# Experts computed only for the tokens that chose them: 32-token slots in four column groups of the array, planned on the chip

## The reference

```python
def _L1_ffn_ref(x, gate_w, routing_bias, w1, w2, w3, sw1, sw2, sw3):
    E = 16; K = 4
    def _swiglu(x, w1, w2, w3):
        a = x @ w1
        return a * jax.nn.sigmoid(a) * (x @ w2) @ w3     # w1, w2: 512 x 1365, w3: 1365 x 512
    gate_out = x @ gate_w + routing_bias
    top_v, top_i = jax.lax.top_k(gate_out, K)
    chosen = jax.nn.one_hot(top_i, E).sum(axis=-2)
    probs = jax.nn.softmax(jnp.where(chosen > 0, gate_out, NEG), axis=-1)
    weights = probs * chosen
    out = _swiglu(x, sw1, sw2, sw3)                       # the shared expert, every token
    for e in range(E):
        out = out + _swiglu(x, w1[e], w2[e], w3[e]) * weights[..., e:e + 1]
    return out
```

## Time and profile before

| | us |
|---|---|
| median of 3 runs | 536.06 |
| profiled execution, device time | 535.71 |
| its span, first to last instruction | 533.7 |
| PE busy / its weight loads | 522.6 / 406.9 |
| DVE / ACT / POOL busy | 425.1 / 337.2 / 8.9 |
| bytes moved | 190.11 MB, mean 356 GB/s |

### The profile page before, as it was taken

One profiled execution on the slowest core, in us unless ns is written; L12 is line 12 of the kernel. 1 busy time (PEld: TensorE's weight loads), 2 busy tenths in 40 slices (PEclk: granted clock), 3 DMA queues, 4 the chain that ended last, 5 costly groups with the idle time before them and its releaser, 6 DMA issues.

```text
span 533.7 us, 7582 instructions
## 1 busy us (share of the span) xinstructions
PE 522.6 (98%) x2672; PEld 406.9 (76%) x2672; DVE 425.1 (80%) x426; ACT 337.2 (63%) x324; POOL 8.9 (2%) x40
## 2 busy tenths in 40 slices
PE   8999799999999999999999999999999999999998
PEld 4665335467878888888888888888888888888886
DVE  6724610167899989889898998989998988989796
ACT  1100100158787878788786877877787877778573
POOL 2000000011000000000000000000000000000000
PEclk9988999999999999999999999999999999999999
DMA  8999999999999999999989999899999999999331
GB/s 338 422 421 421 421 421 422 417 409 416 414 404 414 372 375 348 351 394 337 404 284 380 374 344 384 320 381 339 368 358 356 345 341 395 340 369 350 123 108 70
DMA packets 37032, 190.11 MB, mean 356 GB/s; under 512 B 4090, under 2 KB 4474, under 8 KB 31636
## 3 DMA queue, kind: packets, MB, share of 16 engines
q1 hardware_dynamic: 36816, 189.70, 92.0%
q10 hardware_dynamic: 196, 0.14, 0.1%
HBM read 189.56 MB, written 0.26 MB: 356 GB/s over the span
## 4 chain that ended last, share of the span: by engine, by line
PE 91%; DVE 7%; ACT 1%; issue 1%; DMA 1%; POOL 0%; DVEq 0%; ACTq 0%; POOLq 0%
PE ps L1572 29%; PE ps L1610 23%; PE ps L1576 14%; PE ps L1594 4%; PE ps L1221 3%; PE ps L1385 3%; DVE s_lo L891 2%; PE ps L1414 1%; PE ps L1402 1%; PE ps L1214 1%; PE ps L1283 1%; PE ps L1299 1%; DVE s_lo L903 1%; PE ps L1273 1%; PE ps L1287 1%; PE ps L1545 1%
## 5 line engine op out<-in xcount | busy, mean ns | idle before, releaser
L891 DVE TENSOR_TENSOR s_lo<-w_raw,s_hi 128x1365 fp32r<-128x1365 f32 x136 | 209.1, 1579 | 16.0 <-ACT s_hi L657 15.6
L657 ACT CAST s_hi<-w_raw 128x1365 fp32r<-128x1365 f32 x136 | 180.4, 1337 | 26.3 <-PE ps L1576 13.1
L1572 PE MATMUL ps<-s_hi,xT_hi 128*128 128x512 f32 (+1 forms) x408 | 153.7, 377 | 0.3 <-DVE s_lo L891 0.3
L1572 PE MATMUL ps<-s_lo,xT_hi 128*128 128x512 f32 (+1 forms) x408 | 149.7, 369 | 0.0
L1576 PE MATMUL ps<-s_hi,xT_lo 128*128 128x512 f32 (+1 forms) x408 | 106.6, 369 | 0.0
L903 DVE TENSOR_TENSOR s_lo<-w_raw,s_hi 128x1536 fp32r<-128x1536 f32 x68 | 105.8, 1578 | 0.0
L669 ACT CAST s_hi<-w_raw 128x1536 fp32r<-128x1536 f32 x68 | 90.8, 1343 | 21.4 <-PE ps L1576 18.3
L1572 PEld LDWEIGHTS ps<-s_hi,xT_hi 128*128 128x128 f32 x408 | 76.6, 188 | 17.0 <-DVE s_lo L891 0.5
L1572 PEld LDWEIGHTS ps<-s_lo,xT_hi 128*128 128x128 f32 x408 | 77.0, 189 | 12.5
L1576 PEld LDWEIGHTS ps<-s_hi,xT_lo 128*128 128x128 f32 x408 | 72.7, 189 | 6.0
L1610 PE MATMUL ps<-s_hi,hT_hi 128*128 128x512 f32 (+1 forms) x180 | 72.8, 404 | 0.2 <-DVE hT_lo L1097 0.2
(11 more groups left out here) (249 smaller groups left out, 305.5 us busy)
## 6 DMA issues: line engine op xcount, KB each, us to landing
w_raw<-in_w SPq DMA_DIRECT2D x128, 682.5 KB, 6.2
w_raw<-in_w SPq DMA_DIRECT2D x51, 768.0 KB, 6.1
w_set<-in_w SPq DMA_DIRECT2D x31, 1024.0 KB, 24.5
w_raw<-in_w SPq DMA_DIRECT2D x12, 512.0 KB, 5.8
w_raw<-in_sw SPq DMA_DIRECT2D x8, 682.5 KB, 15.6
wk_sb<-in_wk SPq DMA_DIRECT2D x2, 1024.0 KB, 16.6
wq_sb<-in_wq SPq DMA_DIRECT2D x2, 1024.0 KB, 16.0
gcn_sb<-in_gcn_w SPq DMA_DIRECT2D x2, 1024.0 KB, 13.1
```

Source lines behind the costliest of these rows:

```text
L657: a.copy(s_hi[pair][:, 0:F1], raw[:]).then_inc(hi_ready, 1)
L891: v.tensor_tensor(s_lo[pair][:, 0:F1], raw[:], s_hi[pair][:, 0:F1].bitcast(F32), ALU.subtract).then_inc(lo_ready, 1)
L1572: mm(bank(i + c0 // D)[:, 0:n], xT_hi[:, k], w[:, c0:c0 + n], start=(k == 0 and w is hi), stop=False)
```

## The change

The last stage is written anew, with the rest left nearly as it was.

**Slots.** Work is done in slots of 32 tokens for one expert. Slots 0 to 3 are the shared expert for tokens 0-31, 32-63 and so on. After them come 36 routed slots, always 36: TURNS = 18 turns of two slots, the number that suffices for any choice of the tokens (`most_turns`). A turn has a slot on side b and one on side a.

**The PE work of a slot.** The 1365 columns of w1 and w2 are cut into four groups of 342 (the last is padded from 339 to 342), one for each 32 columns of the array: `up` makes 4 row tiles x 4 groups = 16 matmuls of 32 tokens x 342 for w1, and as many for w2. `down` makes 3 row tiles x 4 groups = 12 matmuls of 512 columns. The four groups' partial sums lie in four sets of 32 PSUM partitions, and `add_slot` adds them and puts them on their tokens with one 128x512 matmul whose stationary operand, `spread`, holds the gates. Everything is fp32; the splitting into hi and lo is gone. `gather_batch` gathers the tokens of four slots at once.

**The weights.** They are used where they land. A ring of two buffers holds one expert each; loads fetch w1 and w2 whole (four DMAs of 128 rows each), and w3 in two: w3a with 128 rows, 16 KB each, and w3b with 86 rows, 8 KB each (342 = 2 x 128 + 86).

**The plan.** On DVE, `router` ranks the logits, and `plan_slots` orders the experts by their number of slots, places 1 to 16. Odd places use side b and buffer 1, even ones side a and buffer 0. A pair of places (1 and 2, 3 and 4, ...) takes as many turns as its odd place has slots. Turns that are left over, `spare`, are put ahead of a pair when loads would be late by its count, and whatever is left goes ahead of the last pair (`pinned`). A table of integers results. PE reads the place of each slot from it into a register and waits until that place's load is there; SP reads for each load which expert to fetch and after which slot (`last_use`) the buffer is free.

The main parts of the diff (sizes, semaphores, SBUF addresses and the removed functions, which the section on the kernel before shows, are left out):

```diff
+SLOT_T = 32
+COL_GROUPS = P // SLOT_T
+CW = -(-F1 // COL_GROUPS)
+TURNS = most_turns()
+ROUTED = 2 * TURNS
+ALL = SHARED + ROUTED
+ring = place("ring", [P, 2, RING], F32, base)
...
+            def load_up(r, part, w):
                 for k in range(KT):
+                    at = (W1_AT, W2_AT)[part] + FW * k
+                    sp.dma_start(ring[:, r % 2, at:at + F1], w[P * k:P * k + P, :]).then_inc(ld_ring[r % 2][part], 16)
+
+            def load_down(r, wa, wb):
+                full = W3_AT + (H_TILES - 1) * COL_GROUPS * D
+                sp.dma_start(ring[:, r % 2, W3_AT:full], wa).then_inc(ld_ring[r % 2][2], 16)
+                sp.dma_start(ring[0:LAST_ROWS, r % 2, full:RING], wb).then_inc(ld_ring[r % 2][2], 16)
...
+            sp.wait_ge(table_ready, 1)
+            for r in range(2, NE):
+                at = ROUTED + r - 2
+                e = sp.value_load(table[0:1, at:at + 1], min_val=1, max_val=E1 - 1)
+                last_use = sp.value_load(table[0:1, at + E1 - 1:at + E1], min_val=SHARED - 1, max_val=ALL)
+                sp.wait_ge(up_ps[0], last_use)
+                load_up(r, 0, one(w1, e))
+                sp.wait_ge(up_ps[1], last_use)
+                load_up(r, 1, one(w2, e))
+                sp.wait_ge(y_slot_ps, last_use)
+                load_down(r, one(w3a, e + 1), one(w3b, e + 1))
...
+            def plan_slots():
...
+                then(v.tensor_tensor(ahead[:], across(order_key), along(order_key), ALU.is_gt))
+                then(v.tensor_reduce(place_no[:], ahead[:], AX_X, ALU.add))
...
+                then(v.tensor_scalar(spare[:, 1:2], spare[:, 0:1], -1.0, float(TURNS), ALU.mult, ALU.add))
+                then(v.tensor_tensor(round_no[:], place_no[:], parity[:], ALU.add))
...
+                then(v.tensor_reduce(earlier[:], matrix, AX_X, ALU.add))
+
+                then(v.scalar_tensor_tensor(lag[:], round_no[:], -2.0, earlier[:], ALU.add, ALU.subtract))
...
+                then(v.tensor_scalar(delay[:], delay[:], spare[:, 1:2], None, ALU.min))
+                then(v.tensor_scalar(pinned[:], round_no[:], float(E1), spare[:, 1:2], ALU.is_ge, ALU.mult))
+                then(v.tensor_tensor(delay[:], delay[:], pinned[:], ALU.max))
+                then(v.tensor_tensor(first_turn[:], delay[:], earlier[:], ALU.add))
...
+            router()
+            gate(0)
+            plan_slots()
+            for i in range(1, ALL + 1):
+                if i % COL_GROUPS == COL_GROUPS - 1 and i // COL_GROUPS < BATCHES:
+                    copy_batch(i // COL_GROUPS + 1)
+                if i < ALL:
+                    gate(i)
+                copy_y(i - 1)
+                if i % COL_GROUPS == 1 and i // COL_GROUPS < BATCHES:
+                    choose_batch(i // COL_GROUPS + 1)
...
+            def up(i, part):
+                to = bank(2 * (i % 2) + part)
+                rows = ex[i // COL_GROUPS % 2]
+                c0 = SLOT_T * (i % COL_GROUPS)
+                for k in range(KT):
+                    for g in range(COL_GROUPS):
+                        at = (W1_AT, W2_AT)[part] + FW * k + CW * g
+                        last = mm(to[SLOT_T * g:SLOT_T * g + SLOT_T, 0:CW], rows[:, k, c0:c0 + SLOT_T],
+                                  ring[:, buffer_of(i), at:at + CW],
+                                  start=(k == 0), stop=(k == KT - 1), skip_group_check=True)
+                last.then_inc(up_ps[part], 1)
...
+            def down(i):
+                pe.wait_ge(hT_ready, i + 1)
+                for t in range(H_TILES):
+                    rows = P if t < H_TILES - 1 else LAST_ROWS
+                    for g in range(COL_GROUPS):
+                        own = slice(SLOT_T * g, SLOT_T * g + SLOT_T)
+                        at = W3_AT + (COL_GROUPS * t + g) * D
+                        last = mm(bank(5)[own], hT[i % 2][0:rows, t, own], ring[0:rows, buffer_of(i), at:at + D],
+                                  start=(t == 0), stop=(t == H_TILES - 1), skip_group_check=True)
+                last.then_inc(y_slot_ps, 1)
...
+            for i in range(ALL + 2):
+                if i < ALL:
...
+                    if i >= SHARED:
+                        pe.wait_ge(here[0], place_now + 1)
...
+                    up(i, 0)
+                if 0 < i <= ALL:
+                    transpose_h(i - 1)
...
+                    spread_gates(i - 1)
+                if i > 1:
+                    add_slot(i - 2)
+                if i < ALL:
...
+                    if i >= SHARED:
+                        pe.wait_ge(here[1], place_now + 1)
+                    up(i, 1)
...
+                if 0 < i <= ALL:
...
+                    if i > SHARED:
+                        pe.wait_ge(here[2], place_then + 1)
+                    down(i - 1)
+                if i % COL_GROUPS == 2 and i // COL_GROUPS < BATCHES:
+                    pe.wait_ge(spread_ready, i)
+                    gather_batch(i // COL_GROUPS + 1)
+                place_then = place_now
+                if SHARED - 1 <= i < ALL - 1:
...
+                    at = i + 1 - SHARED
+                    place_now = pe.value_load(table[0:1, at:at + 1], min_val=1, max_val=E1)
```

More of the change, by code:

```diff
@@ L41, with most_turns @@
 NE = E1 + 1
[L42 to L57, removed]
+SLOT_T = 32
+COL_GROUPS = P // SLOT_T
+CW = -(-F1 // COL_GROUPS)
+FW = COL_GROUPS * CW
+H_TILES = -(-CW // P)
+LAST_ROWS = CW - (H_TILES - 1) * P
+SHARED = P // SLOT_T
+def most_turns():
+    most = 0
+    for cuts in combinations_with_replacement(range(SHARED + 1), E1 - 1):
+        sizes = cuts[::-1]
+        for first in range(SHARED + 1):
+            every = (first, *sizes)
+            fewest = sum(SLOT_T * (n - 1) + 1 for n in every if n)
+            if fewest <= P * K1 <= SLOT_T * sum(every):
+                most = max(most, max(every) + sum(max(n, 1) for n in sizes[1::2]))
+    return most
+TURNS = most_turns()
+ROUTED = 2 * TURNS
+ALL = SHARED + ROUTED
+BATCHES = -(-ROUTED // COL_GROUPS)
+W1_AT, W2_AT, W3_AT = 0, KT * FW, 2 * KT * FW
+RING = W3_AT + H_TILES * COL_GROUPS * D
 SLOTS = 5
-EARLY = 2
 SMALL = (3 * ET, 2 * KT, 4, KT * E0, KT * E1, E1)
 SETS = 2 * GROUPS * CHUNKS0
-PAIRS_N = 6
-SLOT = 3 * D
 LN_EPS = 1e-5
@@ L347, in used_of, with part_ready @@
         return KT * n + t + 1
[L349 to L383, removed]
+    def part_ready(r, part):
+        return (64, 64, 32)[part] * (r // 2 + 1)
     block = nc.Block()
@@ L779, in _, with copy_spread @@
+            def copy_spread(i):
+                act.wait_ge(spread_ps, i + 1)
+                if i > 1:
+                    act.wait_ge(sum_ps, i - 1)
+                a.copy(spread[i % 2][:], bank(7)[:, 0:P]).then_inc(spread_ready, 1)
+            for i in range(ALL + 1):
+                if i < ALL:
+                    silu(i)
+                if i > 0:
+                    copy_hT(i - 1)
+                    copy_spread(i - 1)
         @blk.vector
@@ new lines, in add_slot, with gather_batch @@
+            def add_slot(i):
+                pe.wait_ge(y_slot_ready, i + 1)
+                pe.wait_ge(spread_ready, i + 1)
+                mm(bank(6), spread[i % 2][:], y_sb[i % 2][:], start=(i == 0), stop=(i == ALL - 1)).then_inc(sum_ps, 1)
+            def gather_batch(q):
+                pe.wait_ge(hots_ready, q)
+                for k in range(KT):
+                    last = mm(tiles(7)[:, k], xn[:, P * k:P * k + P], hots[q % 2][:], start=True, stop=True)
+                last.then_inc(batch_ps, 1)
```

647 lines of the change are left out of this document (248 added, 399 removed).

## The result

| | us |
|---|---|
| before, median of 4 runs | 536.05 (535.95 to 536.72) |
| after, median of 4 runs | 913.38 (909.91 to 916.4) |
| ratio after / before, 95% interval | 1.7032 (1.697 to 1.7095) |
| after, the profiled execution and its span | 913.31, 911.6 |
| forecast | 775, range 600 to 815 |

The change makes the kernel 70% slower. The sign is the forecast's, and so is the main cause, a `w3b` carried by two DMA engines; what that costs was mis-sized. The forecast is 138 us short, and the time lies outside its range.

A forecast was written before the change was run, and what follows sets the result against it. PE bounded the old kernel; in the new one PE waits some 225 us for loads. Slot 0 at 133.0, slots and loads to 758.6, the end to 766, 768 with the span's surroundings, plus 7 for the clock: 775 us, range 600 to 815.

The forecast's parts named there:

- the term of `w3b` in the load of an expert: Load of w3b's 86 rows: two engines at 26.3 GB/s each, 13.4 us of the 31.7 us per expert.
- places 9 to 14: Six expert loads without a break, 63 us of load for 20 us of PE per pair, ending at 653.6 us.
- idle turns, places 15, 16: Three spare turns ahead of the last pair, slot 36's w1 ending at 689.8, then 68.8 us of loads to 758.6.
- The start: Before the last stage's slots: last input there at 128.8 us, about 4.2 us of small operations, slot 0 at 133.0.
- The slot: PE's work for one slot of the last stage: 10.1 us, so 404 us for 40 slots.
- the register read: PE's read of the slot's place ahead of each slot: taken as 0.5 us, between 0 and at most about 1.7.
- The plan: Slot order for these tokens: 25 routed slots needed, 36 computed, spare 3, all ahead of the last pair; places 13 and 14 computed four times.
- The clock: PE's lower clock after rests: 1.7 us lost per restart, about four restarts on the path, 7 us.
- A: The forecast itself: w3b carried by two DMA engines, 745 to 815 us; chance 0.72.
- Rival B: w3b's rows spread evenly over the engines, 20 us per expert load, 625 us, range 590 to 655; chance 0.19.
- C: Loads are no bound and PE alone sets the end; 531.5 us at 9.6 us a slot; chance 0.03.
- D: PE runs the slots at 1.2 GHz throughout, a slot of 18 us, 890 us plus waits; chance 0.03.

The follow-up runs named there:

- the loads by themselves: Kernels with all computation left out, only loads issued and awaited, three experts per pattern; 86 rows with eight 128-row loads took 38.1 us per expert.
- rows96: Changed kernel with the load of w3b padded from 86 to 96 rows of zeros; 660.03 us median, 1.2317 of before.
- split80: Changed kernel with the 86-row load of w3b cut into loads of 80 and 6 rows, no padding; 657.71 us median, 1.2256 of before.

## Why the prediction was wrong

The step that failed is the term of `w3b` in the load of an expert: "13.4 us, and these two hold up all later loads". The 13.4 are right for the load alone (15.4 with the landing), and that two engines carry it is right. Wrong is that the others lose only by waiting for them: with eight loads beside it, it costs 22 us (38.1 less 16.0). I had taken 26.3 GB/s per engine as a constant; the one stretch that it came from had all engines on loads of the same kind. That the overlap costs this much is measured; why it does stays open.

The forecast's own steps against the trace; the time at which `down` gets the last `w3b` of each stage:

| step | forecast | measured | more in this step |
|---|---|---|---|
| slot 0 | 133.0 | 143.6 | 10.6 |
| place 2 | 208.8 | 233.5 | 14.1 |
| places 3, 4 | 315.0 | 349.9 | 10.2 |
| places 5, 6 | 400.4 | 458.5 | 23.2 |
| places 7, 8 | 463.7 | 546.3 | 24.5 |
| places 9 to 14 | 653.6 | 783.3 | 47.1 |
| idle turns, places 15, 16 | 758.6 | 902.0 | 13.7 |
| end, with the clock's 7 | 775 | 913.3 | -5.1 |

The rows of `down` that end four of these waits, in the kernel after:

```profile
233.52 4.19 PE L1527 MATMUL ps<-ring,hT 128*32 128x512 f32 x24 [7.47 <-POOLq L544]
...
458.47 1.94 PE L1527 MATMUL ps<-ring,hT 128*32 128x512 f32 x8 [16.28 <-POOLq L544]
...
783.29 4.08 PE L1527 MATMUL ps<-ring,hT 128*32 128x512 f32 x24 [7.52 <-POOLq L544]
...
902.01 4.45 PE L1527 MATMUL ps<-ring,hT 128*32 128x512 f32 x24 [14.98 <-POOLq L544]
```

- **The loads** are about 127 of the 138 us, counting in each step only from its first issue to its last landing. PE's stretches between a landing and the next issue add 6, of these 3.9 before the issue of place 2 (179.5 us, 165.0 forecast) and 3.6 before that of place 5. Places 9 to 14 give 7.9 us an expert, near the 8.7 of the loads by themselves. Not all of that need be the overlap: with 96 rows the same places are 4.5 us an expert over the 20 of even loads. In the kernel the two were not separated; in the loads by themselves the 8.7 stand on top of the eight's own 14.0. In 5 to 8 it is 12 an expert: the loads of place 7 are issued from 438 us on, while the `w3b` of place 6, issued at 412.6, is still under way.
- **The start** is 10.6. The forecast took the last stage's input from the earlier trace rows; there the bias row stood behind two of the shared expert's 0.7 MB loads, now it stands behind all eight and is issued 7.9 us later. The diff moved the other six ahead of it, and of a moved load everything counts that now stands in front. With the row early, slot 0 starts at 132.9.
- **The slot** was 10.1 us in the forecast and is 9.21, with a gather 10.43, in slots 32 to 37: 9.5 in the mean. 0.45 of the 0.6 between is the register read, taken at 0.5 and worth 0.05. It moves the time little, for PE sets the pace only in the first pairs and the idle turns:

```profile
822.66 2.76 PE L1527 MATMUL ps<-ring,hT 128*32 128x512 f32 x24
831.86 2.76 PE L1527 MATMUL ps<-ring,hT 128*32 128x512 f32 x24
841.07 2.76 PE L1527 MATMUL ps<-ring,hT 128*32 128x512 f32 x24
```

- **The plan** was read rightly (the first pair takes as many turns as any expert has slots, here 4, where the section on the change speaks of its odd place). Places 13 and 14 are computed four times: PE runs from 784 to 843 us without a wait, and the load of place 15 is issued only at 818.7; the waits stand at the slots named, and PE waits for VectorE in slot 2, 4.0 us where 6 were forecast.
- **The clock** was underrated in number: half an `up` takes 2.51 us at full clock and 4.3 to 4.8 after a rest, and `down` 4.1 to 5.3 instead of 2.76 (granted 0.5 to 0.6 in the rests, that is the lower level, 1.2 GHz). This follows 16 of the 21 waits for a load, not four; the other five waits are under 0.7 us. Most of it is hidden by the load that follows; where `up` leads to the next issue it adds 2.3 us to the step.
- **The range** took 1.7 to 26.8 us as the ends for `w3b`, the upper one from a single engine, but carried neither that end nor a slowing of the other loads into its own upper end: 815 was A's, 40 us over the forecast. With 26.8 - 13.4 us more on 15 experts, 201 us, it would have been 976.
- **Rival B** (evenly spread, 625) is what rows96 and split80 make: 660 and 658. Taking off the late start leaves 649. The other 24 are in the cadence, 24.5 us per expert and not 20, at 346 GB/s in 480 to 540 us. That is near before's own rate of 359 in 300 to 400, and not the 421 of the first 130 us from which B was worked out. Why the rate is lower there no run shows. Rivals C and D did not come.

No version here beats the kernel before. The best is 611 us, and PE waits 114 us in it: a pair of places holds both buffers until its longer expert is done, so the loads stand still, then run at their limit. An order of one expert after the other, with only one buffer held, was not tried.

## What to carry to other kernels

Before a load's bytes are priced, see how its rows are dealt to the engines: 86 rows went to 2 of 16, and padding them to 96, or cutting them into 80 and 6, took 253 and 256 us from a kernel of 913. A load on few engines costs more than its own time, since it slows what runs beside it; where it can't be spread, issue it when nothing follows at once (28.8 us instead of 38.1 in the loads by themselves). In this kernel `w3b` was already the last load of its expert, but the next expert's loads followed it. And of a small load that a change moves, look at what now stands ahead of it in the queue.

## What the runs showed of the hardware

- A DMA engine's rate was not its own. It was 26 GB/s each when all carry equal loads in the first stages (419 GB/s at a share of 1.01) and for two alone (52 at 0.13), but 22 with equal loads in the kernel with 96 rows from 480 to 540 us (346 at 1.01), 20 for two alone at the end of the kernel after (39 at 0.12), and 15 for each of sixteen while two of them carry an 86-row load (245 at 1.02). A full share of busy engines is thus no sign of a full rate.
- How many engines a load used followed from its number of rows. While only the small load's engines had work, the DMA share was 0.06 with 43 rows, 0.13 with 86, 0.19 with 87, 0.25 with 92 and 0.65 to 0.73 with 88: 1, 2, 3, 4 and 11 of 16.
- SyncE's issue of eight loads took 4 to 6 us with room in the queues, 13 to 34 us behind an 86-row load, and 16 to 21 us behind a backlog of evenly dealt loads too.
- A register read from SBUF on TensorE, ahead of a slot of matmuls, cost at most 0.05 us.
